# Passes over zeros ahead of chunk 0, two gate tiles by turns, chunk 3 taken forward, and adding transfers for w1_lo and w2_lo

## The reference

```python
x = x + attn(layernorm(x))       # pre = x @ W + b, split into i, f, o, z (256 each)
#   i = 10*tanh((i+bias)/10), f = -softplus(f); scan over the 2048 steps of a sequence:
#   m' = max(f+m, i); c = exp(f+m-m')*c + exp(i-m')*tanh(z); n likewise with 1
#   h = sigmoid(o) * c / (n + 1e-6); h / rms(h) * scale
x = x + ffn(layernorm(x))        # layernorm(gamma, beta), w1 = (q1-128)*s1 (256 x 1024),
#   silu(h @ w1 + b1) @ w2 + b2, w2 = (q2-128)*s2 (1024 x 256); x + 0.5 * that
```

## Time and profile before

| | us |
|---|---|
| median of three runs | 319.47 |
| lowest, highest | 318.48, 319.52 |
| profiled execution | 319.09 |
| its span, first to last instruction | 317.0 |
| mean granted TensorE clock | 0.989 |
| busy: PE, PEld | 303.9, 264.5 |
| busy: DVE, ACT, POOL | 269.6, 228.8, 127.2 |

### The profile page before, as it was taken

How to read it: one execution, slowest core, us unless ns; L and a number is a source line. 1 busy time by engine, 2 the same in 40 slices (tenths; PEclk the granted TensorE clock), 3 DMA queues, 4 the chain that set the end, 5 groups by cost and what they waited for, 6 DMA issues and landing times.

```text
span 317.0 us, 4814 instructions
## 1 busy us (share of the span) xinstructions
PE 303.9 (96%) x1760; PEld 264.5 (83%) x1760; DVE 269.6 (85%) x474; ACT 228.8 (72%) x372; POOL 127.2 (40%) x127
## 2 busy tenths in 40 slices
PE   0899999999998999999999999999999999999996
PEld 0788888887996889988899889988899899899896
DVE  3998999999999999999989997879969998764431
ACT  2499965998599866798685968489684966931930
POOL 2053026012196349313950178011999365153000
PEclk9999997899999999999999999999999999999999
DMA  7990000000000130012000200000000100100101
GB/s 265 373 376 17 0 1 0 2 0 0 2 1 0 35 99 3 1 66 68 1 2 33 99 2 0 33 13 23 1 2 0 68 0 0 68 0 15 54 2 66
DMA packets 10951, 14.21 MB, mean 45 GB/s; under 512 B 688, under 2 KB 10160, under 8 KB 10672
## 3 DMA queue, kind: packets, MB, share of 16 engines
q1 hardware_dynamic: 10512, 13.12, 11.8%
q10 hardware_dynamic: 416, 0.79, 0.7%
HBM read 9.71 MB, written 4.19 MB: 44 GB/s over the span
## 4 chain that ended last, share of the span: by engine, by line
PE 65%; DVE 16%; POOL 9%; ACT 5%; issue 2%; DMA 1%; POOLq 0%; DVEq 0%; ACTq 0%
PE mm_ps L219 11%; PE mm_ps L221 11%; PE mm_ps L220 11%; PE z_ps L221 7%; PE z_ps L219 7%; PE z_ps L220 7%; DVE y_lo L776 3%; POOL rows L1068 3%; POOL g L1053 2%; PE t_ps L339 2%; PE t_ps L353 1%; PE t_ps L331 1%; DVE g L744 1%; DVE bn L757 1%; PE z_ps L361 1%
## 5 line engine op out<-in xcount | busy, mean ns | idle before, releaser
L219 PE MATMUL z_ps<-w_hi,y_hi 128*128 128x256 f32 x248 | 70.5, 284 | 0.0
L221 PE MATMUL z_ps<-w_hi,y_lo 128*128 128x256 f32 x248 | 69.9, 282 | 0.0
L220 PE MATMUL z_ps<-w_lo,y_hi 128*128 128x256 f32 x248 | 69.8, 281 | 0.0
L776 DVE TENSOR_TENSOR y_lo<-y,y_hi 128x512 fp32r<-128x512 f32 x64 | 44.6, 711 | 8.6 <-ACT y_hi L506 8.4
L503 ACT ACTIVATE y<-mm_ps,b_all 128x512 f32<-128x512 f32 x60 | 41.2, 687 | 13.0 <-PE mm_ps L288 11.1
L220 PEld LDWEIGHTS z_ps<-w_lo,y_hi 128*128 128x128 f32 x248 | 46.8, 189 | 0.3
L219 PEld LDWEIGHTS z_ps<-w_hi,y_hi 128*128 128x128 f32 x248 | 46.6, 188 | 0.4
L221 PEld LDWEIGHTS z_ps<-w_hi,y_lo 128*128 128x128 f32 x248 | 46.7, 188 | 0.0
L219 PE MATMUL mm_ps<-gt_hi,w_hi 128*128 128x512 f32 x108 | 43.7, 404 | 0.0
L220 PE MATMUL mm_ps<-gt_lo,w_hi 128*128 128x512 f32 x108 | 43.0, 398 | 0.0
L221 PE MATMUL mm_ps<-gt_hi,w_lo 128*128 128x512 f32 x108 | 42.8, 396 | 0.0
(11 more groups left out here) (156 smaller groups left out, 672.9 us busy)
## 6 DMA issues: line engine op xcount, KB each, us to landing
out<-rows SPq DMA_DIRECT2D x15, 256.0 KB, 2.1
rows<-x SPq DMA_DIRECT2D x7, 512.0 KB, 6.7
q<-fc_q SPq DMA_DIRECT2D x2, 1024.0 KB, 12.2
s<-fc_scales SPq DMA_DIRECT2D x1, 1024.0 KB, 11.5
wg_raw<-fc_scales SPq DMA_DIRECT2D x1, 1024.0 KB, 11.0
wg_raw<-w_gates SPq DMA_DIRECT2D x1, 512.0 KB, 5.6
wg_raw<-w_gates ACTq DMA_DIRECT2D x1, 512.0 KB, 6.1
rows<-x ACTq DMA_DIRECT2D x1, 256.0 KB, 3.6
```

The source lines that it names most:

```text
L219: pe.matmul(dst, wh[w_at], ah[a_at], start=start, stop=False)
L220: pe.matmul(dst, wh[w_at], al[a_at], start=False, stop=False)
L221: return pe.matmul(dst, wl[w_at], ah[a_at], start=False, stop=stop)
L776: dve.tensor_tensor(y_lo[:, j], y[:, j % YBUFS], y_hi[:, j].bitcast(F32), ALU.subtract).then_inc(y_lo_done, 1)
```

## The change

It has four parts.

- **Passes over zeros.** VectorE zeroes `gt_hi[:, 0]` first of all; TensorE then makes 16 matmuls of 512 columns over it before the transposes of chunk 0 and 4 more behind them. Their output is never read.
- **The first two gate tiles by turns.** `first_two_gates` makes for each half k the hi*hi passes of both tiles, then the lo*hi of both, and the passes with `xt_lo` last, so that `wg_lo` and `xt_lo` are waited for later.
- **Chunk 3 forward.** ln1(3) is put ahead of mean_square(0), x_normalised(3) is laid between ScalarE's gates of chunk 2, x_turned(3) ahead of `shifted_bias`, and gates(3, 0..1) ahead of fc1(0). The banks and the buffer waits are changed for that, and chunk 3's tanh of the i tiles goes into `xn`. ScalarE's reciprocal(1) and silu(0) stand behind those tiles.
- **w1_lo and w2_lo.** The two subtractions on VectorE go. GpSimd writes -w_hi into w_lo (`negated`, one 128x2048 instruction each), and a transfer issued from GpSimd adds w_f to it in memory (`whole_added`). The negation of w1 stands behind h(0) and ahead of ln1_root(3) and rms_root(0); that of w2 behind the first half of `gt_hi` of chunk 0. The scaling of w2 moves from behind x_low(3) of old to right behind ln2(0); on VectorE the cast of w1_hi moves behind x_low(1).

```diff
             if c == 1 and j in Z_TILES:
                 return z_bank(j - Z_TILES[0])
+            if c == 3 and j < 4:
+                return mm_ps[:, 2 + j % 2]
             return mm_ps[:, (j + 2) % 4 if c == 2 or (c == 1 and j in O_TILES) else j % 4]
 
         def fc1_bank(c, j):
             if c == 0 and j in (4, 5):
                 return z_bank(j - 4)
-            return mm_ps[:, j % 4 if c > 0 or j >= 6 else (j + 2) % 4]
...
@@ -228,10 +233,14 @@
                         pass
                     elif c == 1 and j in O_TILES:
                         pe.wait_ge(gate_done, at(1, 8, j - 5))
+                    elif c == 3 and j < 2:
+                        pe.wait_ge(gate_done, at(2, 8, j + 5))
+                    elif c == 3 and j < 4:
+                        pe.wait_ge(silu_done, at(0, 8, j + 1))
+                    elif c == 3 and j < 6:
+                        pe.wait_ge(silu_done, at(0, 8, j + 3))
                     elif j >= 4:
                         pe.wait_ge(gate_done, at(c, 8, j - 3))
-                    elif c == 3 and j < 2:
-                        pe.wait_ge(silu_done, at(0, 8, j + 3))
...
-                        if c == 0:
-                            pe.wait_ge(wg_split_lo, k + 1)
...
+            def first_two_gates():
+
+                x_hi, x_lo = xt(0)
+                f = [slice(GATE_ORDER[j] * P, GATE_ORDER[j] * P + P) for j in range(2)]
+                for k in range(KD):
+                    pe.wait_ge(xt_hi_done, k + 1)
+                    pe.wait_ge(wg_split_hi, k + 1)
+                    for j in range(2):
+                        pe.matmul(gate_bank(0, j), wg_hi[:, k, f[j]], x_hi[:, k], start=(k == 0), stop=False)
+                    pe.wait_ge(wg_split_lo, k + 1)
+                    for j in range(2):
+                        pe.matmul(gate_bank(0, j), wg_lo[:, k, f[j]], x_hi[:, k], start=False, stop=False)
+                for j in range(2):
+                    for k in range(KD):
+                        pe.wait_ge(xt_lo_done, k + 1)
+                        ins = pe.matmul(gate_bank(0, j), wg_hi[:, k, f[j]], x_lo[:, k], start=False,
+                                        stop=(k == KD - 1))
+                    ins.then_inc(pre_done, 1)
...
                     elif c == 0 and j >= 6:
                         pe.wait_ge(silu_done, at(0, 8, j - 5))
+                    elif c == 0 and j < 2:
+                        pe.wait_ge(gate_done, at(2, 8, j + 7))
+                    elif c == 0:
+                        pe.wait_ge(gate_done, at(3, 8, j - 1))
...
-                            pe.wait_ge(w1_ready, 1)
+                            pe.wait_ge(w1_ready, 16)
...
-                            pe.wait_ge(w2_ready, 1)
+                            pe.wait_ge(w2_ready, 16)
...
-                    elif c >= 3:
+                    elif c == 3:
+                        pe.wait_ge(hs_done, at(0, 4, 2 * k + 2))
+                    elif c > 3:
...
-                    pe.wait_ge(hs_done, at(c, 4, 2 * k + 2))
+                    if c == 0:
+                        pe.wait_ge(xt_lo_done, at(3, 2, k + 1))
+                    else:
+                        pe.wait_ge(hs_done, at(c, 4, 2 * k + 2))
...
-                    if exists(c + 2):
+                    if exists(c + 2) and c != 1:
...
+            def idle_passes(count):
+                for _ in range(count):
+                    pe.matmul(mm_ps[:, 3], gt_hi[:, 0, 0:P], gt_hi[:, 0], start=True, stop=True)
+
+            pe.wait_ge(zeros_ready, 1)
+            idle_passes(IDLE_PASSES)
             pe.wait_ge(ident_ready, 2)
...
+            idle_passes(IDLE_PASSES // 4)
+
+            first_two_gates()
+            gates(0, range(2, 5))
             x_turned(1)
...
             gates(2, range(0, 2))
             h_turned(0)
             gates(2, range(2, GJ))
+            x_turned(3)
             shifted_bias()
             g_turned(0)
-            fc1(0, range(0, 6))
-            x_turned(3)
-            fc1(0, range(6, KF))
             gates(3, range(0, 2))
+            fc1(0, range(KF))
             h_turned(1)
             gates(3, range(2, GJ))
             fc2(0, range(0, 3))
...
+            def capped(c):
+
+                return xn[:].rearrange("p t d -> p (t d)").rearrange("p (k m) -> p k m", m=T) if c == 3 else rec[c % 2][:, 1]
...
+                if c == 4:
+                    act.wait_ge(i_ready, at(3, 1, 1))
...
             gates(2, I_TILES)
             square_sums(0)
-            gates(2, range(2, GJ))
+            gates(2, range(2, 3))
+            for n in range(TT):
+                gates(2, range(n + 3, n + 4))
+                x_normalised(3, range(n, n + 1))
+            gates(2, range(7, GJ))
+            x_high(3)
             g_normalised(0)
             g_high(0)
+            gates(3, I_TILES)
             act.preload_act_table_set("natural_log_exp_and_others")
+            exp_i(2)
             reciprocal(1)
-            exp_i(2)
-            x_normalised(3)
             act.preload_act_table_set("silu_and_others")
             act.wait_ge(b1_ready, 1)
-            silu(0, range(0, 2))
-            x_high(3)
-            silu(0, range(2, 4))
+            silu(0, range(0, 4))
             silu_alone(0, range(4, KF))
-
-
-            gates(3, range(0, 1))
             square_sums(1)
-            gates(3, range(1, 2))
             act.preload_act_table_set("sigmoid_and_others")
             gates(3, range(2, GJ))
...
+            dve.memset(gt_hi[:, 0].bitcast(F32), 0.0).then_inc(zeros_ready, 1)
             dve.memset(minus_half[:], -0.5).then_inc(half_ready, 1)
...
             dve.wait_ge(s1_in, 16)
             dve.scalar_tensor_tensor(out=w1_f, in0=q1[:], scalar=-ZERO_POINT, in1=s1[:],
                                      op0=ALU.add, op1=ALU.mult).then_inc(w1_scaled, 1)
+            maximum(0, range(KD))
+            x_low(1)
             dve.wait_ge(w1_scaled, 1)
             dve.tensor_copy(w1_hi[:, 0], w1_f[:, 0]).then_inc(w1_rounded, 1)
-            maximum(0, range(KD))
-            x_low(1)
             denominators(0, range(KD))
             divisor(0)
             numerators(0)
@@ -841,36 +889,34 @@
             x_low(2)
             h(0)
 
-            dve.wait_ge(w1_rounded, KD)
-            dve.tensor_tensor(w1_lo[:], w1_f, w1_hi[:].bitcast(F32), ALU.subtract).then_inc(w1_ready, 1)
-            maximum(1, range(0, 1))
+            ln1(3)
             mean_square(0)
-            ln1_sums(3)
             dve.wait_ge(row_in, 16)
             h_scaled(0)
             residual(0)
             ln2_sums(0)
             ln2(0)
-            ln1_means(3)
-            maximum(1, range(1, KD))
-            denominators(1, range(KD))
+            dve.wait_ge(q2_in, 16)
+            dve.wait_ge(s2_in, 16)
+            dve.scalar_tensor_tensor(out=w2_f, in0=q2[:], scalar=-ZERO_POINT, in1=s2,
+                                     op0=ALU.add, op1=ALU.mult).then_inc(w2_scaled, 1)
+            x_low(3)
+            maximum(1, range(KD))
             dve.wait_ge(beta_w1, 1)
             dve.tensor_tensor(b1_all[:], z_ps[:, 0, 0, 0:KF], col[:, COL_B1:COL_B1 + KF], ALU.add
                               ).then_inc(b1_ready, 1)
+            denominators(1, range(0, 1))
+            g_low(0)
+            denominators(1, range(1, KD))
             divisor(1)
-            g_low(0)
             numerators(1)
             o_times_c(1)
             newton(1)
             refined(1)
             h(1)
+            y_low(0, range(0, 1))
             input_times_z(2)
-            y_low(0, range(0, 2))
-            x_low(3)
-            dve.wait_ge(q2_in, 16)
-            dve.wait_ge(s2_in, 16)
-            dve.scalar_tensor_tensor(out=w2_f, in0=q2[:], scalar=-ZERO_POINT, in1=s2,
-                                     op0=ALU.add, op1=ALU.mult).then_inc(w2_scaled, 1)
+            y_low(0, range(1, 2))
             y_low(0, range(2, 4))
...
             mean_square(1)
             ln1_sums(4)
-            dve.wait_ge(w2_rounded, 1)
-            dve.tensor_tensor(w2_lo[:], w2_f, w2_hi[:].bitcast(F32), ALU.subtract).then_inc(w2_ready, 1)
             h_scaled(1)
...
+            def negated(lo, hi, done):
+                pool.tensor_scalar(lo[:], hi[:].bitcast(F32), -1.0, 0.0, ALU.mult, ALU.add).then_inc(done, 1)
+
+            def whole_added(lo, whole, done, ready):
+                pool.wait_ge(done, 1)
+                pool.dma_start(lo[:], whole, accum_op=ALU.add).then_inc(ready, 16)
...
+            pool.wait_ge(w1_rounded, KD)
+            pool.wait_ge(h_done, at(0, 1, 1))
+            negated(w1_lo, w1_hi, w1_negated)
+            ln1_root(3)
             rms_root(0)
+            whole_added(w1_lo, w1_f, w1_negated, w1_ready)
             pool.wait_ge(x1_done, at(0, 1, 1))
             input_times_z(1)
             ln2_root(0)
-            ln1_root(3)
             pool.wait_ge(w2_scaled, 1)
             pool.tensor_copy(w2_hi[:], w2_f).then_inc(w2_rounded, 1)
+            pool.wait_ge(w2_rounded, 1)
```

(4 more changed lines are left out.)

15 lines of the change are left out of this document (8 added, 7 removed).

## The result

The changed kernel takes 316.46 us (median of four runs, 316.21 to 317.67) against 319.15 for the kernel before on the same chip: 0.9931 times as long, 95% interval 0.9914 to 0.9947. Two later comparisons gave 0.9917 (0.9894 to 0.9941) and 0.9919 (0.9902 to 0.9935). So the change takes 2.3 to 2.7 us away, where the prediction had it add 1.5. The profiled execution was the longest of its four: 317.67 us, span 315.9 (before: 319.09 and 317.0). Both are used, since they differ in one thing that matters.

A forecast was written before the change was run, and what follows sets the result against it. The prediction took VectorE's chain until about 103 us, with a port shared with GpSimd, to bound the kernel. +0.55 us up to h_scaled(0) and +0.95 in the middle gave +1.5, so 320.6 us, range 316.5 to 323.0.

The forecast's parts named there:

- The start: Up to chunk 0's denominators: TensorE gains 0.9 us, but the denominators start at 26.15 instead of 25.85, +0.3 us.
- w1_lo: Up to h_scaled(0): GpSimd's negation, taken as 2.4 us, delays the roots; h_scaled(0) at 43.85 instead of 43.31, +0.55 so far.
- the removed 2.29 us turn into waiting: Before h_scaled(0): VectorE loses w1's subtraction at 38.55 but then only waits, so nothing is gained.
- The middle: VectorE from h_scaled(0) to h_scaled(1): operations taken out, brought in and blocked sum to +0.95 us.
- The cast's block: GpSimd's cast of w2 falls on chunk 1's scans and blocks VectorE 2.2 us instead of 1.7: +0.5 us.
- the term +2.3: GpSimd's negation of w2_hi, about 56 us, gets the port during VectorE's SBUF scans and blocks it 2.3 us.
- rival (2): Blocks of w2's negation and cast fall beside VectorE's PSUM operations: 318.3 to 316.1, taken as 317.2 us; chance 0.27.
- The sum: +0.55 and +0.95 give +1.5 us on VectorE's chain at 103 us; span 317.0 becomes 318.5, time 320.6 us.
- (1): GpSimd's product of chunk 0 gets the port between the two scans, at 21.7 us: 1.2 us more, 321.8; chance 0.19.
- (3): At the start the clock doesn't hold after the passes: denominators at 26.6, +0.45 us, 321.1; chance 0.11.
- (4): The w1 transfer is late and TensorE stands 8 us at fc1(0): about 326 us; chance 0.06.
- theory A: From the experiments: VectorE's chain, with the port shared with GpSimd, sets the end until 102 us; TensorE's lead alone is worthless.

The follow-up runs named there:

- e1_after_again: The changed kernel run again with no edit; 316.44 us, its profiled execution with a span of 314.4 us.
- e15_after_same_chip: The changed kernel unaltered, run once more for comparison on one chip beside the versions with w2's rounding in ScalarE's gaps; 316.41 us.
- the next version: The changed kernel with w2's rounding and negation in halves, the rounding in ScalarE's gaps, and w2's scaling behind the first maximum scan and x_low(3); 315.15 us.

## Why the prediction was wrong, step by step

**Which engine sets the end: right.** From `h_scaled(1)` to `xt_lo` of chunk 4 VectorE takes 21.88 us before, 21.87 after and 21.87 in e1_after_again. What it gains before 80 us arrives at 102 us and at the end whole (1.2 and 1.1 us; 2.6 and 2.6). The span ends 214.5 to 214.7 us behind the start of that `xt_lo` in 16 of the 17 profiled executions, whatever was edited ahead of it, and 214.3 in the one without the passes.

**The start: +0.3 forecast, -0.33 found.** TensorE's part was right to 0.1 us. The order of scans, product, cast and denominators was as forecast; its sizes were not. The scans end 0.12 us earlier than assumed (22.83), the product then takes 2.2 us and not 2.5, and from its end at 25.04 to the denominators it is 0.48 us, not the cast's full 0.69: together the 0.63 us between 26.15 and 25.52. The Trainium skill's exclusive lock ("SBUF — State Buffer", section "SBUF: two separate sides") held on each row shown of this stretch.

**w1_lo: +0.25 forecast between the denominators and `h_scaled(0)`, -0.06 found** (25.52 to 42.92 is 17.40, 25.85 to 43.31 was 17.46). The step "the removed 2.29 us turn into waiting" was right: VectorE stands 0.89 and 1.40 us there, 2.29 us in all. The negation was mis-sized: 1.92 us where I took 2.4 by the cast's 2.29. That cast was itself a blocked row; unblocked it takes 1.89. And more than the negation bounds the wait: `mean_square(0)` stands for ScalarE's squares until 41.35 us, and GpSimd's root for it starts at 41.79, so a negation shorter by more than 0.2 us would not have brought `h_scaled(0)` forward.

**The middle: +0.95 forecast, -0.78 and -2.02 found.** Taken out and brought in as listed: -0.55, -2.2, +1.2. The cast's block was put at 2.2 and is 1.69, as before, so +0.5 falls to 0. The negation of w2 was put at 2.3; it is 1.5 in the profiled execution and 0.3 in e1_after_again. VectorE's waits shrink by 0.5 (busy 36.13 of 37.20 us before, 35.87 of 36.42 after, 34.63 of 35.18), not 0.3. That gives -0.55 - 2.2 + 1.2 + 0 + 1.5 - 0.5 = -0.55, and -1.75 with 0.3. Taken from start to start instead, waits and small rows together shrink by 0.74 us: the first y_low by 0.38, `gt_lo` by 0.23 (1.53 to 1.30), `divisor` by 0.21, the sum of the bias by 0.12, while the two denominators scans grow by 0.20 beside their block. With that the sum closes, at -0.79 and -1.99. The step that failed most is the term +2.3, the negation that "gets the port at a handover" and blocks VectorE for its whole length: the negation of w2 blocks 1.5 us in one execution and 0.3 in the usual ones. I had its start within 0.4 us, named its other case as rival (2), and gave the main weight to an order that hangs on 0.1 to 0.35 us. By itself it takes the sum from +1.5 to -0.5 in the usual order and to +0.7 in that of the profiled execution; the cast's block (+0.5, found 0), the start and w1 bring the rest.

**The sum.** -0.33 - 0.06 - 0.78 = -1.2 us for the profiled execution; e1_after_again has `h_scaled(0)` 0.56 us earlier than before and so -0.56 - 2.02 = -2.6. Forecast was +1.5. Of the 4.1 us between +1.5 and -2.6, 2.5 are blocks by GpSimd's two passes over w2, 1.1 the start and w1 together, and 0.4 the waits and small rows.

**The rivals.** (1) did not happen in the change, but it is what its start does by itself, and what the moved cast prevents (320.76 and 318.33): its deciding point, which side of a scan the request falls on, was named rightly. (2), a block hidden beside `gt_lo`, is what happened in the usual case, for the negation alone; I gave it 317.2 us and a chance of 0.27, and its far end 316.1. The cast's block, which it also would have hidden, is there in full (1.69 us), so that the time comes near its far end is owed to the start, w1 and the waits as well. (3) The clock held: pitch 0.23 us at 10.28, the level of 2.4 GHz, behind 0.31 us of standing, eight transposes and four passes. What the Trainium skill says of transposes ("TensorE: Matmul & The Clock Gate", section "Part 4: PE-mode transpose": they don't count as busy) speaks for rival (3); over this stretch the clock did not fall. No run here parts the transposes from the passes around them, so the rule itself stays untested. (4) The transfers landed in 7.0 and 7.6 us. That of w1 was issued at 43.8 us and TensorE's first pass with `w1_lo` is at 59.6, so 8 us were to spare.

**Other readings.** The root for g was held as said (3.01 us), and TensorE waited 1.2 us for g, where 1 was forecast. That I counted this at nothing was right for this kernel and wrong for the next version: it is the second chain of the middle. The half clock I said would stay; in 50 to 55 us the granted clock is 0.97 after and 0.65 before, and in 55 to 60 us 0.69. The 32 narrow matmuls now stand ahead of TensorE's wait for g, and the clock falls at about 54.7 us, some 3 us later than before (51.5), during the transposes of g; it is back at 58.1 (58.3 before). In e1_after_again the low stretch is 53.6 to 57.0 us, in e15_after_same_chip 52.6 to 59.4. By theory A it brought nothing to the end by itself, but when it falls decides the order at the port:

```profile
50.00:55.00 5.00, 3.83 (x33) 3.75 (x33) 5.00 (x5) 2.49 (x6) 3.62 (x3) 0.97 0.00 0
55.00:60.00 5.00, 5.00 (x18) 4.05 (x17) 5.00 (x6) 2.27 (x4) 3.02 (x2) 0.69 0.13 26
```

What is not settled: why the clock falls 1 to 2 us earlier in one execution than in another with the same work, and whether the second chain by itself would have paid.

## What to carry to other kernels

Where two engines can't work at the same time on one memory, the price of an operation moved to the second is not its length but what stands on the first when it is asked for: look at the next boundary, and if it is within half a microsecond, give both outcomes as cases with like chances. Look also at what sets the moment of the request: here it was the clock of a third engine. Before a row's duration is used as a length, see whether it stood for the port itself. And a freed engine pays only as far as the next chain behind it: look at every engine, and free two level chains together.

## What the runs showed that I had not expected

- Who gets the port is a matter of 0.1 us: a GpSimd request at 21.45 inside the first of two scans got in between them (pair 4.57 us), one at 21.68, about 0.1 us inside the second, waited for its end (pair 2.45 us).
- VectorE's batch statistics take no part, though all their operands lie in SBUF: those at 45.87 us take their own 1.41 us under GpSimd's product of 45.93, and the negation at 38.46 its own 1.92 beside those at 38.22. The prediction's rule, "whose operands all lie in SBUF", is too wide by them, though its sum rightly left them unblocked.
- GpSimd's cast and its negation of 128x2048 elements take 1.89 and 1.92 us; ScalarE's take 1.90 and 1.91.
- An adding transfer of 1 MB from SBUF to SBUF, issued from GpSimd, held that engine 0.95 to 1.06 us and landed in 7.3 us, where loads of 1 MB at the start took 12.2.
